# A decoder layer on one core: keys, values and both C products in another order on TensorE and VectorE

## The chip, the core and the metric

The kernel runs on one core of a Trainium2 chip. A core has five engines with a queue each, which work through their own instructions in order and meet only at semaphores: TensorE (PE) for matrix products into the eight PSUM banks, VectorE (DVE), ScalarE (ACT), GpSimd (POOL), and SyncE (SP), which here issues the transfers. TensorE's clock has two levels, 1.2 and 2.4 GHz. The metric is device time in microseconds (us), the median of several runs.

## The reference

One decoder layer over x of 8 x 256 tokens by 256 features, in three parts. The change lies in the first, which is the state-space mixer and the projections of the attention:

```python
x = _lin(x, w1); x = _depthwise_conv(x, conv_w, conv_b); x = jax.nn.silu(x)
x_delta = jax.nn.softplus(_lin(x, dl_w, dl_b))
A_bar = jnp.exp(-x_delta * _lin(x, A_w, A_b))
h = jnp.cumsum(_lin(x, B_w, B_b) * jnp.cumprod(A_bar, axis=1), axis=1)
ssm_out = _lin(h, C_w, C_b) + _lin(x, D_w, D_b)
z = ssm_out * jax.nn.silu(_lin(ssm_out, w2))
out = ssm_out + _lin(z, w3)
...
x = x + _L0_attn_ref(_layernorm(x, axis=-1), ...)
x = x + _L0_xattn_ref(_layernorm(x, axis=-1), ctx_1024, ctx_1024, ...)   # q from x, k and v from the context
x = x + _L0_ffn_ref(_layernorm(x, axis=-1), ...)
```

## The kernel before

The kernel has three stages, one after the other with a barrier between them: the mixer and the projections to queries, keys and values (`mixer_and_projections`), the attention, and the output projection with routing and experts. Queries, keys and values go to DRAM at the end of the first stage and are loaded again by the second.

The first stage works in four blocks of 512 tokens (`NBLK`, i = 0 to 3), with 256 features as two halves of 128 partitions. Each fp32 operand is split in a high and a low part (fp32r), and `split_product` makes three matmuls of each product. ScalarE as a rule writes the high part with an ACTIVATE, and VectorE or GpSimd the low part by a subtraction. The block loop is a software pipeline, written out by hand for each engine: iteration i does the work of block i (`now`) and what is left of block i - 1 (`last`), and the queries of block i - 2. There is no planner: the order of the calls in these loops is the order of the instructions.

On TensorE an iteration has the twelve chunks of dl, A and B of block i through a ring of four banks, `direct`, `turn_x` and `w1` of the next block, `w2` of the last, `turn_c` (transposes of the context), and then the part that the change reorders: `w3(i - 1)`, whose 40 matmuls also add the mixer's sum by an identity; `keys(i)` (12 matmuls of 512 columns); `values(i)` (24 of 256); `mixed(i, 0)` and `mixed(i, 1)`, the two halves of the product with C (12 of 512 each); and `turn_q(i - 1)`, the transposes of the normalised x that becomes the query input. `queries(i - 2)` then follows in the next iteration, behind the first two chunks.

The other engines meet this part so:

- VectorE adds w3's product to x (`residual`), makes the statistics of the second layer norm (`statistics`), the low part of keys (`biased_low`), the normalised x (`normed`), adds the bias to values (`value`), makes the running sum over the product with C (`summed`, a scan) and the low part of the turned x (`x2_low`), which stands between the two halves of the sum.
- GpSimd makes the reciprocal root of the variance (`power`, L329). Then come the remainders of values for their split in three bf16 parts (`v_rest`, L359, and `v_third`, L363), and in the next iteration `ssm_sum` (L339) and `dmin` (L334).
- ScalarE makes the high part of keys (`k_high`), the first and second parts of values (`v_first`, `v_second`) and then the high part of the turned x (`x2_high`, L537). Its next exponential, `exp` (L467), waits for a chunk of the ring.

Banks 4 to 7 are used as two pairs in turn. Which pair a product takes follows from its place in the tuple `PAIRS`. Before a pair is written, the reader of what was in it before must be done, so the order of the products also says which waits stand ahead of each.

Of the kernel before, what the change touches and what calls it, by code (L numbers as in the profile page):

```python
# [15 lines left out]
B, L, D = 8, 256, 256  # L16
N = B * L
DC = D // P
# [148 lines left out]
PAIRS = ("Q", "T", "D", "W1", "W2", "TC", "W3", "K", "V", "C", "TQ")  # L167


def mixer_and_projections(nc, sems, c, x_sb, wo, bo, a, disp, qd, kd, vd):  # L170

    with ExitStack() as ctx:
# [71 lines left out]
        with nc.Block() as block:  # L244
# [385 lines left out]
            def _(pe):  # L630
# [54 lines left out]
                def mixed(i, m):  # L685
                    pe.wait_ge(S["gh"], HC * (i + 1))
                    pe.wait_ge(S["gl"], HC * (i + 1))
                    pe.wait_ge(S["kl"], DC * (i + 1))
                    split_product(pe, pair(i, "C", m)[:, :], products("C_w", m, (gh, gl))).then_inc(S["C"], 1)
# [11 lines left out]
                def w3(i):  # L701
# [3 lines left out]
                    pe.wait_ge(S["zl"], DC * (i + 1))  # L705
                    for n in range(2):
# [16 lines left out]
                def keys(i):  # L723
                    if i == 0:
                        split_done(pe, "WQ")
                    pe.wait_ge(S["ch"], DC * (i + 1))
                    pe.wait_ge(S["cl"], DC * (i + 1))
                    for m in range(DC):
                        split_product(pe, pair(i, "K", m)[:, :], products("WK", m, (xbh, xbl))).then_inc(S["k"], 1)

                def values(i):
                    ge(pe, S["x_out"], 2 * i)
# [17 lines left out]
                for i in range(NBLK + 2):  # L750
# [20 lines left out]
                    if now:  # L771
                        chunk(i, "B", 1)
                        chunk(i, "dl", 3)
                        chunk(i, "A", 3)
                        turn_c(i)
                        chunk(i, "B", 2)
                        chunk(i, "B", 3)
                    if last:
                        w3(i - 1)
                    if now:  # L780
                        keys(i)
                        values(i)
                        mixed(i, 0)
                    if last:
                        turn_q(i - 1)
                    if now:
                        mixed(i, 1)

            @block.vector
            def _(dve):  # L790
# [161 lines left out]
                for i in range(NBLK + 2):  # L952
# [43 lines left out]
                    if now:  # L996
# [4 lines left out]
                        weighted(i, 3)  # L1001
                    if last:
# [4 lines left out]
                    if now:  # L1007
                        biased_low(i, "K", bk, i)
                    if last:
                        normed(i - 1)  # L1010
                    if now:
                        value(i, 0)
                        value(i, 1)
# [791 lines left out]
```

## Time and profile before

| | us |
|---|---|
| median of 3 runs (lowest, highest) | 880.38 (880.03, 880.54) |
| the profiled execution | 886.03 |
| its span | 884.3 |
| TensorE busy in the span | 693.3 (78%) |
| VectorE, ScalarE, GpSimd busy | 578.6, 434.1, 370.6 |

The profile is one execution with the hardware profiler on. Its time is some 6 us above the median of the runs. "Span" runs from the first to the last instruction. The first stage fills the first 285 us of it, and the attention's first matmul is at 316.79 us. A row of the timeline gives start and length in us, engine, line, operation, output and inputs by the program's names, the shape, and how often it repeats; in brackets the idle time of the engine before it and the instruction that ended it. Matmuls are pipelined, so their starts are read, and not their ends.

### The profile page before, as it was taken

Reading aid. Unit: us, or ns where it says so; the run is one execution under the profiler, and the core shown is the slowest. Engines: PE = TensorE matmul, PEld = TensorE weight load, DVE = VectorE, ACT = ScalarE, POOL = GpSimd, SP = SyncE. Lnnn points to the kernel's source line nnn. Section 1 sums busy time; section 2 is a strip of 40 time slices with the busy share of each in tenths; the row PEclk is TensorE's granted clock in tenths of the full one; section 3 lists DMA queues with packets and bytes.
Section 4 is the critical chain, followed back from the end, with each engine's and each line's share of the span. In section 5 each row is a group of like instructions: output and inputs, shape, how many; then the busy total and the mean of one; then the engine's idle time right before and its main releaser. Section 6 shows DMA issues by size and latency. Waiting matters only on the chain. (4 is left out here: it accounts for less than half of the span.)

```text
span 884.3 us, 15113 instructions
## 1 busy us (share of the span) xinstructions
PE 693.3 (78%) x4776; PEld 607.0 (69%) x4792; DVE 578.6 (65%) x1269; ACT 434.1 (49%) x971; POOL 370.6 (42%) x338
## 2 busy tenths in 40 slices
PE   3767969799765068898888676516999999999992
PEld 2556858688644046666666575516999999999992
DVE  6574466574753049999999767713777787777741
ACT  4554646535341047777777512103565565555641
POOL 1429456364420300000000156671466866866756
PEclk9788979989997569999999856556999999999997
DMA  9002005511030242121111052215044354251213
GB/s 302 19 25 86 1 24 212 190 65 69 23 111 30 90 139 51 47 46 47 47 46 41 19 197 73 70 43 186 2 136 113 60 147 131 39 146 19 28 22 41
DMA packets 54858, 70.36 MB, mean 80 GB/s; under 512 B 10843, under 2 KB 45542, under 8 KB 54800
## 3 DMA queue, kind: packets, MB, share of 16 engines
q1 hardware_dynamic: 45584, 61.82, 21.7%
q0 software_dynamic: 9216, 7.81, 6.2%
q8 instruction: 31, 0.51, 0.2%
q14 instruction: 27, 0.22, 0.1%
HBM read 42.57 MB, written 28.79 MB: 81 GB/s over the span
## 5 line engine op out<-in xcount | busy, mean ns | idle before, releaser
L1115 ACT ACTIVATE a_pr<-a_scores,a_nm 128x128 f32<-128x128 f32 (+1 forms) x256 | 90.5, 426 | 81.9 <-DVE a_nm L1187 78.6
L1695 DVE SCALAR_TENSOR_TENSOR w_v<-w_th,w_bank 128x324 f32<-128x324 f32 x128 | 63.0, 492 | 70.5 <-ACT w_th L1425 69.2
L1564 PE MATMUL w_bank<-w_w2h,w_hh 128*108 128x256 f32 x384 | 108.5, 283 | 0.5 <-POOL w_hl L1350 0.5
L1564 PE MATMUL w_bank<-w_w2h,w_hl 128*108 128x256 f32 x384 | 107.7, 280 | 0.0
L1564 PE MATMUL w_bank<-w_w2l,w_hh 128*108 128x256 f32 x384 | 107.4, 280 | 0.0
L1425 ACT ACTIVATE w_th<-w_bank 128x324 f32<-128x324 f32 x128 | 56.6, 442 | 100.0 <-PE w_bank L102 99.8
L1350 POOL TENSOR_TENSOR w_hl<-w_v,w_hh 128x324 fp32r<-128x324 f32 x64 | 56.4, 882 | 91.4 <-ACT w_hh L1431 91.4
L1184 DVE TENSOR_REDUCE a_mx<-a_scores 128x2 f32<-128x512 f32 (+1 forms) x96 | 65.5, 682 | 35.6 <-remote 34.1
L1366 POOL IOTA w_x<- 128x16 uint32 x1 | 0.2, 190 | 208.0 <-POOLq L1078 208.0
L102 PE MATMUL w_bank<-w_xh,w_w1h 128*128 128x324 f32 x256 | 81.1, 317 | 1.1 <-ACT w_xh L1420 1.1
L102 PE MATMUL w_bank<-w_xh,w_w1l 128*128 128x324 f32 x256 | 80.8, 316 | 0.0
L102 PE MATMUL w_bank<-w_xl,w_w1h 128*128 128x324 f32 x256 | 80.6, 315 | 0.0
L1150 PE MATMUL a_turned<-c_ident,a_pr 128*128 128x128 f32 x384 | 61.1, 282 | 21.0 <-ACT a_pr L1115 19.7
L1671 DVE TENSOR_TENSOR w_w2l<-w_s,w_w2h 128x256 fp32r<-128x256 f32 x64 | 74.3, 1160 | 2.2
L102 PE MATMUL a_scores<-a_kxh,a_qh 128*128 128x512 f32 x96 | 47.3, 493 | 33.5 <-DMA a_vs<-vd 33.5
L1192 DVE TENSOR_TENSOR a_pl<-a_turned,a_ph 128x512 f16<-128x512 f32 x96 | 66.4, 692 | 6.5 <-ACT a_ph L1122 5.7
L1564 PEld LDWEIGHTS w_bank<-w_w2h,w_hh 128*108 128x108 f32 x384 | 65.9, 172 | 0.7 <-issue 0.7
L1431 ACT ACTIVATE w_hh<-w_v 128x324 fp32r<-128x324 f32 x128 | 60.4, 472 | 12.0 <-DVE w_v L1695 11.2
L1564 PEld LDWEIGHTS w_bank<-w_w2l,w_hh 128*108 128x108 f32 x384 | 66.0, 172 | 0.0
L1564 PEld LDWEIGHTS w_bank<-w_w2h,w_hl 128*108 128x108 f32 x384 | 65.8, 171 | 0.0
L1150 PEld LDWEIGHTS a_turned<-c_ident,a_pr 128*128 128x128 f32 x384 | 43.6, 143 | 30.9 <-ACT a_pr L1115 27.2
L102 PE MATMUL m_bank<-m_sh,m_wh 128*128 128x512 f32 x112 | 48.0, 429 | 19.5 <-ACT m_sh L458 6.9
(230 smaller groups left out, 2031.2 us busy)
## 6 DMA issues: line engine op xcount, KB each, us to landing
w_s<-in_L_ffn_w SPq DMA_DIRECT2D x16, 1024.0 KB, 5.9
disp<-c_blank SPq DMA_DIRECT2D x8, 658.1 KB
w_rows<-disp SPq DMA_DIRECT2D x8, 658.1 KB
vd<-m_vs SPq DMA_DIRECT2D x4, 816.0 KB, 3.7
a_vs<-vd SPq DMA_DIRECT2D x1, 3264.0 KB, 11.8
g_x<-in_x SPq DMA_DIRECT2D x4, 512.0 KB, 7.7
m_cin<-in_ctx SPq DMA_DIRECT2D x4, 512.0 KB, 5.0
kd<-m_qkh SPq DMA_DIRECT2D x4, 512.0 KB, 2.9
```

The costliest lines, as they stand in the source:

```text
L102: mm = pe.matmul(out, a, b, start=first and n == 0, stop=last and n == 3 * len(parts) - 1)
L1115: ins = act.activation(pr[:, u % 2, j * n:(j + 1) * n], sbank[u % 3][:, j * n:(j + 1) * n], ACT.Exp, bias=nm[:, u, j:j + 1], scale=SCALE)
L1150: mm = pe.transpose(tbank[u % 3][:, j * P:(j + 1) * P], pr[:, u % 2, j * P:(j + 1) * P], c["ident"][:, :])
L1184: dve.tensor_reduce(mx[:, u, 0:nh], sbank[u % 3][:, :].rearrange("p (h k) -> p h k", h=nh), AX.X, ALU.max).then_inc(S["mx"], 1)
L1192: dve.tensor_tensor(pl[:, u % 3, :], tbank[u % 3][:, :], ph[:, u % 3, :], ALU.subtract)\
L1350: pool.tensor_tensor(hl[:, g % 3, half(1)], v[:, n % 4, :], hh[:, g % 3, half(1)].bitcast(F32), ALU.subtract)\
L1366: pool.iota(x3[:, :, TOK:TOK + 1].bitcast(U32), [[P, NT], [1, 1]], base=0, channel_multiplier=1)\
L1425: act.activation(th[:, n % 2, :], hb[n % 3][:, 0:HALF], ACT.Tanh, scale=0.5).then_inc(F["th"], 1)
L1431: act.activation(hh[:, g % 3, half(u)], v[:, n % 4, :], ACT.Copy).then_inc(F["hh"], 1)
L1564: mm = pe.matmul(eb[t // 2][0:SP_, (t % 2) * D:(t % 2 + 1) * D], a[:, g % 3, s], w2_piece(b, f), start=f == 0 and t % 2 == 0 and n == 0, s ...
L1671: dve.tensor_tensor(w2_piece(w2l, f), w2_piece(s2[e % 2], f), w2_piece(w2h, f).bitcast(F32), ALU.subtract)\
L1695: dve.scalar_tensor_tensor(v[:, n % 4, :], th[:, n % 2, :], 1.0, hb[n % 3][:, 0:HALF], ALU.add, ALU.mult).then_inc(F["v"], 1)
```

## The change

Four edits in the first stage. The tuple `PAIRS` names keys and values ahead of w3's product. On TensorE `keys(i)` and `values(i)` stand ahead of `w3(i - 1)`, and `mixed(i, 1)` ahead of `turn_q(i - 1)`. On VectorE the low part of keys and the two value sums stand ahead of the residual, and the normalisation follows the statistics directly. Waits follow the banks: C waits for the value sums (`vf`) and no longer for the low part of keys (`kl`), w3's product waits for `kl`, keys wait for `z`, and values no longer wait for `x_out`.

```diff
--- before.py
+++ after.py
@@ -164,7 +164,7 @@
 HIGH_ORDER = ("w1", "dl_w", "A_w", "B_w", "D_w", "WQ", "w2", "WO")
 LOW_VECTOR = ("w1", "dl_w", "A_w", "B_w", "D_w")
 LOW_GPSIMD = ("WQ", "w2", "WO")
-PAIRS = ("Q", "T", "D", "W1", "W2", "TC", "W3", "K", "V", "C", "TQ")
+PAIRS = ("Q", "T", "D", "W1", "W2", "TC", "K", "V", "W3", "C", "TQ")
 
 
 def mixer_and_projections(nc, sems, c, x_sb, wo, bo, a, disp, qd, kd, vd):
@@ -685,7 +685,7 @@
                 def mixed(i, m):
                     pe.wait_ge(S["gh"], HC * (i + 1))
                     pe.wait_ge(S["gl"], HC * (i + 1))
-                    pe.wait_ge(S["kl"], DC * (i + 1))
+                    pe.wait_ge(S["vf"], 2 * (i + 1))
                     split_product(pe, pair(i, "C", m)[:, :], products("C_w", m, (gh, gl))).then_inc(S["C"], 1)
 
                 def w2(i):
@@ -703,6 +703,7 @@
                         pe.wait_ge(S["identr"], 1)
                     pe.wait_ge(S["zh"], DC * (i + 1))
                     pe.wait_ge(S["zl"], DC * (i + 1))
+                    pe.wait_ge(S["kl"], DC * upto(i + 2))
                     for n in range(2):
                         for j in range(2):
                             tok = slice((2 * n + j) * P, (2 * n + j + 1) * P)
@@ -725,11 +726,11 @@
                         split_done(pe, "WQ")
                     pe.wait_ge(S["ch"], DC * (i + 1))
                     pe.wait_ge(S["cl"], DC * (i + 1))
+                    ge(pe, S["z"], DC * i)
                     for m in range(DC):
                         split_product(pe, pair(i, "K", m)[:, :], products("WK", m, (xbh, xbl))).then_inc(S["k"], 1)
 
                 def values(i):
-                    ge(pe, S["x_out"], 2 * i)
                     pe.wait_ge(S["dx"], DC * (i + 1))
                     for n in range(2):
                         for j in range(2):
@@ -775,16 +776,16 @@
                         turn_c(i)
                         chunk(i, "B", 2)
                         chunk(i, "B", 3)
+                    if now:
+                        keys(i)
+                        values(i)
                     if last:
                         w3(i - 1)
                     if now:
-                        keys(i)
-                        values(i)
                         mixed(i, 0)
+                        mixed(i, 1)
                     if last:
                         turn_q(i - 1)
-                    if now:
-                        mixed(i, 1)
 
             @block.vector
             def _(dve):
@@ -999,18 +1000,17 @@
                         weighted(i, 2)
                         running(i, 3)
                         weighted(i, 3)
+                    if now:
+                        biased_low(i, "K", bk, i)
+                        value(i, 0)
+                        value(i, 1)
                     if last:
                         residual(i - 1, 0)
                         residual(i - 1, 1)
                         dve.wait_ge(S["x_out"], 2 * i)
                         statistics(st2, mom2, ve2, TPB * (i - 1), TPB * i)
-                    if now:
-                        biased_low(i, "K", bk, i)
-                    if last:
                         normed(i - 1)
                     if now:
-                        value(i, 0)
-                        value(i, 1)
                         summed(i, 0)
                     if i == NBLK - 1:
                         last_sum(i, 0)
```

TensorE in the program, from the end of block 1's last chunks on (iteration i = 2): what it issues at the head of each product, before. `m_xbh` is the context's high part, `m_zh` that of z, `m_gh` that of the scan that is multiplied with C, `m_xn` the normalised x, `m_xah` the query input, `m_sh` the input of the chunks.

```order
L715 MATMUL m_bank4<-m_wh,m_zh 128x256 [waits m_zl,m_zh]
...
L102 MATMUL m_bank6<-m_xbh,m_wh 128x512 [waits m_cl,m_ch]
...
L102 MATMUL m_bank4<-m_wh,m_xbh 128x256 [waits m_dx,m_x_out]
...
L102 MATMUL m_bank6<-m_gh,m_wh 128x512 [waits m_kl,m_gl,m_gh]
...
L636 MATMUL m_bank4<-c_ident,m_xn 128x128 [waits m_xn2,m_vf]
...
L102 MATMUL m_bank7<-m_gh,m_wh 128x512 [waits m_kl,m_gl,m_gh]
...
L102 MATMUL m_bank6<-m_xah,m_wh 128x512 [waits m_hs,m_xl2,m_xh2]
```

And now:

```order
L102 MATMUL m_bank4<-m_xbh,m_wh 128x512 [waits m_z,m_cl,m_ch]
...
L102 MATMUL m_bank6<-m_wh,m_xbh 128x256 [waits m_dx]
...
L716 MATMUL m_bank4<-m_wh,m_zh 128x256 [waits m_kl,m_zl,m_zh]
...
L102 MATMUL m_bank6<-m_gh,m_wh 128x512 [waits m_vf,m_gl,m_gh]
...
L102 MATMUL m_bank7<-m_gh,m_wh 128x512 [waits m_vf,m_gl,m_gh]
...
L636 MATMUL m_bank4<-c_ident,m_xn 128x128 [waits m_xn2,m_vf]
...
L102 MATMUL m_bank6<-m_xah,m_wh 128x512 [waits m_hs,m_xl2,m_xh2]
```

The product with w3 has moved behind keys and values, and the second C product ahead of the query transposes. Two chunks stand between the last two rows of each list, as before.

VectorE in iteration i = 3, before: `L900` is the residual, `L810` the statistics, `L915` the low part of keys, `L907` the normalisation, `L922` the value sums, `L894` the scan over C, `L820` the low part of the query input.

```order
L900 TENSOR_TENSOR g_x<-m_bank6,g_x 128x512 [waits m_w3]
...
L810 BN_STATS m_st2<-g_x 128x6 [waits m_x_out]
...
L915 SCALAR_TENSOR_TENSOR m_qkl<-m_bank4,m_bk,m_qkh 128x512 [waits m_kh]
...
L907 TENSOR_SCALAR m_xn<-g_x,m_mom2,m_rstd2 128x256 [waits m_xT,m_rstd]
...
L922 TENSOR_TENSOR m_vf<-m_bank6,m_bv 128x512 [waits m_v3,m_v]
...
L894 SCALAR_TENSOR_TENSOR m_ssm<-m_bank4,m_dx 128x256 [waits m_wlp,m_z,m_dx,m_ssml,m_C]
...
L820 TENSOR_TENSOR m_xal<-m_bank6,m_xah 128x512 [waits m_xh2]
...
L894 SCALAR_TENSOR_TENSOR m_ssm<-m_bank5,m_dx 128x256 [waits m_wlp,m_z,m_dx,m_ssml,m_C]
```

The same place now, with lines one higher:

```order
L916 SCALAR_TENSOR_TENSOR m_qkl<-m_bank6,m_bk,m_qkh 128x512 [waits m_kh]
...
L923 TENSOR_TENSOR m_vf<-m_bank4,m_bv 128x512 [waits m_v3,m_v]
...
L901 TENSOR_TENSOR g_x<-m_bank6,g_x 128x512 [waits m_w3]
...
L811 BN_STATS m_st2<-g_x 128x6 [waits m_x_out]
...
L908 TENSOR_SCALAR m_xn<-g_x,m_mom2,m_rstd2 128x256 [waits m_xT,m_rstd]
...
L895 SCALAR_TENSOR_TENSOR m_ssm<-m_bank4,m_dx 128x256 [waits m_wlp,m_z,m_dx,m_ssml,m_C]
...
L821 TENSOR_TENSOR m_xal<-m_bank6,m_xah 128x512 [waits m_xh2]
...
L895 SCALAR_TENSOR_TENSOR m_ssm<-m_bank5,m_dx 128x256 [waits m_wlp,m_z,m_dx,m_ssml,m_C]
```

Keys' low part and the value sums have moved ahead of the residual. The second scan still stands behind the low part of the query input. The queues of ScalarE, GpSimd and SyncE are the same in both kernels.

## Rows read from the trace of the kernel before

**Rows 1.** The page, part 2: TensorE's granted clock in 40 slices, in tenths.
```profile
PEclk9788979989997569999999856556999999999997
```

**Rows 2.** Timeline of TensorE, block 2: first matmul of each product in turn.
```profile
178.59 0.55 PE L715 MATMUL m_bank<-m_wh,m_zh 128*128 128x256 f32 x1 [5.83 <-POOL m_zl L343]
...
185.27 0.39 PE L102 MATMUL m_bank<-m_xbh,m_wh 128*128 128x512 f32 x1
...
188.05 0.28 PE L102 MATMUL m_bank<-m_wh,m_xbh 128*128 128x256 f32 x1
...
190.90 0.39 PE L102 MATMUL m_bank<-m_gh,m_wh 128*128 128x512 f32 x1
...
193.71 1.04 PE L636 MATMUL m_bank<-c_ident,m_xn 128*128 128x128 f32 x8
...
197.39 0.40 PE L102 MATMUL m_bank<-m_sh,m_wh 128*128 128x512 f32 x1
...
200.20 0.41 PE L102 MATMUL m_bank<-m_xah,m_wh 128*128 128x512 f32 x1
```

**Rows 3.** Timeline of VectorE and GpSimd, low parts of context and z, block 2.
```profile
177.16 1.29 DVE L820 TENSOR_TENSOR m_xbl<-m_bank,m_xbh 128x512 fp32r<-128x512 f32 x2 [3.75 <-ACT m_xbh L512]
...
175.95 2.49 POOL L343 TENSOR_TENSOR m_zl<-m_z,m_zh 128x512 fp32r<-128x512 f32 x2
```

**Rows 4.** Timeline of VectorE, 185 to 199 us.
```profile
185.47 0.69 DVE L900 TENSOR_TENSOR g_x<-m_bank,g_x 128x512 f32<-128x512 f32 x1 [1.62 <-PE m_bank L720]
...
189.73 1.38 DVE L907 TENSOR_SCALAR m_xn<-g_x,m_mom,m_rstd 128x256 f32<-128x256 f32 x4
...
195.96 1.29 DVE L820 TENSOR_TENSOR m_xal<-m_bank,m_xah 128x512 fp32r<-128x512 f32 x2 [0.78 <-ACT m_xah L537]
...
197.59 1.27 DVE L894 TENSOR_TENSOR_SCAN m_ssm<-m_bank,m_dx 128x256 f32<-128x256 f32 x2 [0.34 <-PE m_bank L102]
```

**Rows 5.** Timeline of GpSimd, 188 to 195 us.
```profile
188.57 1.04 POOL L329 TENSOR_TENSOR m_rstd<-m_ve,c_mhalf 128x4 f32<-128x4 f32 x1 [1.25 <-DVE m_ve L119]
192.49 2.28 POOL L359 TENSOR_TENSOR m_vf<-m_vf,m_vs 128x512 f32<-128x512 f32 x2 [2.87 <-ACT m_vs L527]
```

**Rows 6.** Timeline of ScalarE, 182 to 206 us.
```profile
182.83 0.63 ACT L484 ACTIVATE m_gh<-m_acc 128x512 fp32r<-128x512 f32 x1 [0.50 <-DVE m_acc L873]
...
194.79 0.66 ACT L531 ACTIVATE m_vs<-m_vf 128x512 bf16<-128x512 f32 x1 [0.45 <-POOL m_vf L359]
195.35 1.06 ACT L537 ACTIVATE m_xah<-m_bank 128x512 fp32r<-128x512 f32 x2
...
204.61 0.69 ACT L467 ACTIVATE m_e<-m_bank,m_dlb 128x512 f32<-128x512 f32 x1 [0.71 <-PE m_bank L102]
```

**Rows 7.** Timeline of TensorE, C and query products of blocks 1 and 3.
```profile
135.25 0.39 PE L102 MATMUL m_bank<-m_gh,m_wh 128*128 128x512 f32 x1
...
144.54 0.41 PE L102 MATMUL m_bank<-m_xah,m_wh 128*128 128x512 f32 x1
...
242.07 0.39 PE L102 MATMUL m_bank<-m_gh,m_wh 128*128 128x512 f32 x1
...
250.17 0.47 PE L102 MATMUL m_bank<-m_xah,m_wh 128*128 128x512 f32 x1 [1.45 <-DVE m_ssm L894]
```

**Rows 8.** Timeline of VectorE, block 3: the two sums of scan and direct part.
```profile
246.37 1.23 DVE L806 TENSOR_TENSOR m_ssm<-m_ssm,m_dx 128x512 f32<-128x512 f32 x1
...
250.06 0.69 DVE L806 TENSOR_TENSOR m_ssm<-m_ssm,m_dx 128x512 f32<-128x512 f32 x1
```

**Rows 9.** Windows from S on: stretch, its length, busy engines, clock, transfers.
```profile
122.06:128.35 6.29, 6.29 (x30) 6.29 (x31) 4.66 (x7) 2.94 (x5) 2.97 (x3) 0.51 0.01 3
...
178.59:182.95 4.36, 4.36 (x20) 4.36 (x21) 3.95 (x6) 2.42 (x5) 1.58 (x1) 0.51 0.01 4
...
230.17:234.20 4.03, 4.03 (x21) 4.03 (x22) 3.79 (x6) 1.26 (x2) 1.25 (x1) 0.58 0.01 2
```

**Rows 10.** Timeline of VectorE and TensorE: end of the stage, start of the attention.
```profile
284.00 0.75 DVE L915 SCALAR_TENSOR_TENSOR m_qkl<-m_bank,m_bq,m_qkh 128x512 fp32r<-128x512 f32 x1 [0.78 <-ACT m_qkh L544]
...
316.79 0.76 PE L102 MATMUL a_scores<-a_kxh,a_qh 128*128 128x512 f32 x1 [33.55 <-DMA a_vs<-vd]
```

## The prediction

> **What bounds the kernel now.** I read the page first, then the timeline of each engine from 120 to 285 us, since the change touches only the four blocks of the first stage. The clock row of the page shows that this stage is not full: TensorE's granted clock dips in it again and again [rows 1]. The timeline shows a repeating pattern. In block 2 TensorE stands still until 178.59 us, released by GpSimd's last low part of z, and then runs without a gap: product with w3 to 185.27, keys to 188.05, values to 190.90, first C product to 193.71, query transposes, second C product, then two chunks of the next block at 197.39 and the query product at 200.20 [rows 2]. I call the first matmul of such a stretch S and the start of C in the old order W. In blocks 1 and 2 TensorE stays gapless beyond the query product, and ScalarE's next exponential waits for the chunk behind it (204.61, released by PE) [rows 6]. So a microsecond lost between S and the query product is lost for the block. From the third chunk on the block is a chain over ScalarE, VectorE and GpSimd that moves rigidly with its start. After block 3 the query product of block 2 waits outright for VectorE's scan (250.17, idle 1.45) [rows 7], and everything to the end of the stage is serial; attention's first matmul comes 32 us after the last low query part [rows 10], behind stores, a barrier and loads, which move with it.
>
> **What could start sooner: nothing.** Keys and values now go first in the stretch. Keys need the context's low part; the product with w3 needed z's low part. In block 2 VectorE ends the first at 177.16 + 1.29 = 178.45, GpSimd the second at 175.95 + 2.49 = 178.44 [rows 3]. S stays where it is (to 0.05 us), and the idle time ahead of it is not touched. The new wait of keys for z is met: z's low part is made from z. The work from S to W is the same 76 matmuls in another order, so W stays too: 178.59 to 190.90 = 12.31 us [rows 2].
>
> The new wait of w3's product for the low part of keys: the pair of banks that keys fill is the one w3 takes next. ScalarE evicts keys only behind its last copy of g, which ends 182.83 + 0.63 = 183.46, S + 4.87 [rows 6]; two evictions at the 0.69 of the same form [rows 6], and one low part at about the 0.69 of VectorE's 128x512 from a bank [rows 4], with handovers, give S + 7.0. The w3 product takes 6.68, of which 4.36 at half the clock [rows 2, 9], so at full clock 2.32 + 2.18 = 4.5, and it would start at W - 4.5 = S + 7.8. Behind it are queued both C products and the transposes; the margin is 0.8 us. Cost 0 to 0.5, taken 0. The C products now wait for the value sums, which are made while w3's product runs: nothing.
>
> **What becomes later.** The end of w3's product moves from S + 6.68 to W (190.90). It starts this chain, with the spans of block 2:
> - residual, statistics, variance on VectorE, then the power on GpSimd: from the product's end at 185.27 to 188.57 + 1.04 = 189.61 [rows 2, 4, 5], 4.34 us. So W + 4.35.
> - GpSimd's queue is unchanged, and in it the power stands AHEAD of the two value remainders. In the old order these waited for values and began at 192.49, long after the power [rows 5]. Now values are ready first and sit behind the power: 2.25 for the two [rows 5], W + 6.6.
> - ScalarE's second value part waits for the second remainder, and the copies of the turned query input stand behind it: 194.79, then 195.35; VectorE's low parts of the same 195.96 to 197.25 [rows 4, 6]. From the remainders' end (194.75) to the low parts' end 2.5: W + 9.1.
> - VectorE makes the second scan behind these low parts, 1.27 [rows 4]: W + 10.4. The query product waits for it.
>
> In the old order that scan waited only for the second C product, and the query product began at W + 9.30 in block 2 and W + 9.29 in block 1 [rows 2, 7]. TensorE could have it at W + 9.3 now too: C, C, transposes, two chunks are the same work. The transposes alone are checked separately: the last normalised tile is ready at W + 4.35 + 1.38 = W + 5.8 [rows 4], and two C products of 2.81 end at W + 5.6 [rows 2]: 0.1 to 0.2, which disappears in the later wait. So each of blocks 1 and 2 loses 10.4 - 9.3 = 1.1 us. GpSimd's first minimum for the next block comes 2.4 later, but the exponential that waits for TensorE comes only about 1.3 later, and the next one, behind TensorE's third chunk, 1.1.
>
> Block 3 has no chunks behind it. There the query product began at 250.17 - 242.07 = W + 8.10 [rows 7]. Between the scans VectorE also has a sum over two SBUF tensors, 1.23 beside GpSimd's value parts and 0.69 without [rows 8]. It would now start at W + 7.0, where GpSimd again makes those parts (W + 6.6 to 8.9), so I take 1.23: it ends at 8.3, 0.35 past the point at which the first low part could start. W + 10.75, a loss of 2.65. A page of the Trainium skill, "SBUF — State Buffer", section "Who interferes with whom", says that a VectorE instruction with two SBUF inputs contends with a GpSimd one that reads SBUF, under an exclusive lock. The pair of durations agrees.
>
> What is gained: the keys' store leaves sooner, and nothing waits for it; the second C product ends 0.8 sooner (the transposes no longer lie ahead of it), and that is what the longer chain hides.
>
> **The sum.** 1.1 + 1.1 + 2.65 = 4.85 us. The profiled execution took 886.03 us (span 884.3) and would take 890.9; the median of the runs is 880.38, so the same sum gives 885.2.
>
> **The clock.** The stretches at 1.2 GHz after S are 6.3 us long in block 1 and about 4.4 and 4.0 in the others [rows 9]; each costs up to half its length, whichever product lies in it. The change moves work, not the gap before S, so I take 0. Bounds: without any such stretch W could come no sooner than S + 7.0 + 4.5 = S + 11.5 because of the wait for keys; against 13.19, 12.31 and 11.90 now [rows 2, 7, 9] that is at most 1.7 + 0.8 + 0.4 = 2.9 gained. At the long stretch in all three, (6.3 - 4.4)/2 + (6.3 - 4.0)/2 = 2.1 lost. The Trainium skill, "TensorE: Matmul & The Clock Gate", section "What's actually happening", adds that the gate's phase varies from run to run and that one should not fit to a cold count; three lengths in one trace agree, and the term stays 0.
>
> **Rivals.**
> 1. The chain costs nothing (not slower). Place: GpSimd between the power and the remainders of blocks 1 to 3. If the power were ready in time, or the second scan did not have to follow the low parts, the query product would come at W + 9.3, and in block 3 0.8 sooner than now, since C ends 0.8 sooner. It decides for this side once the low parts end before W + 8.0, instead of 9.1. Time 880.38 - 0.8 = 879.6; with half of the clock's possible gain 878.2. Against it: the sequence stands in the queues, with measured spans. 7 in 100.
> 2. The chain costs what I say, and the clock falls in the holes it opens: TensorE idles 1.1 in two blocks and, in block 3, from about W + 6.7 to W + 10.75, where it idled 1.45 before. The query product and the one with w2, some 2.8 us each, could run at half speed: +2.8 to +5.6, of which I take 2.8: 888.0. For it: each longer idle ahead of S ends at half clock [rows 9]. Against it: it needs the hole to be counted as idle. 13 in 100.
> 3. The normalisation on VectorE now meets the remainders on GpSimd. The page on SBUF named above says that a `tensor_scalar` can enter a mode that takes the shared ports, and then one blocks the other. As a mechanism here: the remainders or the normalised tiles come up to 1.38 later [rows 4], three times up to 1.3: +2 to +4, 888. Against it: 1.38 for four tiles of 256 columns, 0.35 each, is no faster than a plain pass of that shape by the 0.69 for 512 from a bank [rows 4]. 7 in 100.
> 4. The chain is shorter than I sum it, or the clock gives back some: a loss of 1 to 3 us, 882.5. 18 in 100.
>
> The forecast itself, 885.2, has 55 in 100, with a range of its own of 883.5 to 887. What a measurement of this kernel tells from no change is 0.2%, 1.8 us. Slower by more: 55 + 13 + 7 and most of rival 4, 0.89. Within: 0.08. Faster: 0.03, rival 1 with clock luck. The range, from the floor of chain less clock (880.4 + 4.85 - 2.9 = 882.3) to rivals 2 and 3: 882 to 888.3.
>
> **What would show it.** Right: S of block 1 unchanged near 122; keys, values, w3's product, C, C, transposes without a gap; the value remainders directly behind the power on GpSimd; the query product waiting about 1 us for VectorE's scan in blocks 1 and 2, and nearly 4 us in block 3; S of blocks 2 and 3 about 1.1 and 2.2 later; the last query part 4.85 later, and equal distances behind it. Wrong: no idle time ahead of the query product; a gap between values and w3's product released by the low part of keys; gaps ahead of S that shrink; remainders that run before the power.

## The result and the profile after

| | before | after |
|---|---|---|
| median (lowest to highest), us | 880.2 (879.84 to 880.54), 4 runs | 901.74 (899.95 to 903.35), 4 runs |
| the profiled execution, us | 886.03 | 902.52 |
| its span, us | 884.3 | 900.8 |

The changed kernel takes 1.0244 times as long, with a 95% interval of 1.0222 to 1.0266. It is slower, as forecast, but by 21.5 us in the medians where the prediction had 4.85. The profiled pair differs by 16.5 us, mostly since before's profiled execution lay 5.8 above its own median. Below, traces are compared with traces and medians with medians.

The whole loss of the traces lies in the first stage. The last product of queries starts at 298.12 us, against 278.81 before, the last low part at 303.42 against 284.00 [rows 10], and attention's first matmul at 335.76 against 316.79 [rows 10]. That is 19.3, 19.4 and 19.0 us. What follows the attention's first matmul is 2.5 us shorter in the later trace, which makes the 16.5 of the pair; a comparison of two single traces is uncertain by some microseconds in total, and is read below place by place.

The timeline of TensorE in block 2 answers to [rows 2]. Columns: start and length in us, engine, line, operation, output and inputs, shape and count, idle time before it and what ended it.

```profile
182.79 0.76 PE L102 MATMUL m_bank<-m_xbh,m_wh 128*128 128x512 f32 x1 [5.78 <-ACT m_xbh L512]
188.04 0.42 PE L102 MATMUL m_bank<-m_wh,m_xbh 128*128 128x256 f32 x1
191.25 0.28 PE L716 MATMUL m_bank<-m_wh,m_zh 128*128 128x256 f32 x1
195.91 0.40 PE L102 MATMUL m_bank<-m_gh,m_wh 128*128 128x512 f32 x1
201.69 0.30 PE L636 MATMUL m_bank<-c_ident,m_xn 128*128 128x128 f32 x1
202.76 0.33 PE L636 MATMUL m_bank<-c_ident,m_xn 128*128 128x128 f32 x1 [0.77 <-DVE m_xn L908]
203.92 0.33 PE L636 MATMUL m_bank<-c_ident,m_xn 128*128 128x128 f32 x1 [0.83 <-DVE m_xn L908]
205.07 0.76 PE L636 MATMUL m_bank<-c_ident,m_xn 128*128 128x128 f32 x5 [0.83 <-DVE m_xn L908]
205.59 0.56 PE L102 MATMUL m_bank<-m_sh,m_wh 128*128 128x512 f32 x1
210.02 0.39 PE L102 MATMUL m_bank<-m_xah,m_wh 128*128 128x512 f32 x1
```

Keys, values, w3's product and the C products follow one another as forecast. S to W, by the prediction's names, is 182.79 to 195.91. But the query product starts at W + 14.11, not W + 10.4. Two things stand between. The eight transposes wait for VectorE's normalised tiles one by one, so that the chunks start 9.68 behind C and not 6.5. And the two chunks take 4.43 instead of 2.81. The reason for the first is on VectorE and GpSimd, in the same stretch (they answer to [rows 4] and [rows 5]):

```profile
196.11 0.69 DVE L901 TENSOR_TENSOR g_x<-m_bank,g_x 128x512 f32<-128x512 f32 x1 [1.65 <-PE m_bank L721]
200.29 4.72 DVE L908 TENSOR_SCALAR m_xn<-g_x,m_mom,m_rstd 128x256 f32<-128x256 f32 x4 [1.15 <-POOL m_rstd L329]
204.94 1.26 DVE L895 TENSOR_TENSOR_SCAN m_ssm<-m_bank,m_dx 128x256 f32<-128x256 f32 x2
206.12 1.26 DVE L821 TENSOR_TENSOR m_xal<-m_bank,m_xah 128x512 fp32r<-128x512 f32 x2
207.30 1.25 DVE L895 TENSOR_TENSOR_SCAN m_ssm<-m_bank,m_dx 128x256 f32<-128x256 f32 x2
```

```profile
199.22 1.04 POOL L329 TENSOR_TENSOR m_rstd<-m_ve,c_mhalf 128x4 f32<-128x4 f32 x1 [7.65 <-DVE m_ve L119]
200.23 2.32 POOL L359 TENSOR_TENSOR m_vf<-m_vf,m_vs 128x512 f32<-128x512 f32 x2
202.51 2.36 POOL L363 TENSOR_TENSOR m_vs<-m_vf,m_vs 128x512 bf16<-128x512 f32 x2
206.27 1.28 POOL L339 TENSOR_TENSOR m_ssm<-m_ssm,m_dx 128x512 f32<-128x512 f32 x1 [1.41 <-DVE m_ssm L895]
```

Four normalised tiles that took 1.38 before [rows 4] take 4.72. They fill the very time in which GpSimd makes its four value remainders (200.23 to 204.87), while GpSimd keeps its pace (2.32 and 2.36, before 2.28 [rows 5]). By source line, all 16 tiles of a run, with lowest, median and highest ns, before and then after:

```profile
L907 DVE TENSOR_SCALAR m_xn<-g_x,m_mom,m_rstd x16: 404/409/414, 134.1 to 275.6; 128x256 f32<-128x256 f32 x16
```

```profile
L908 DVE TENSOR_SCALAR m_xn<-g_x,m_mom,m_rstd x16: 406/1235/1251, 139.1 to 294.9; 128x256 f32<-128x256 f32 x16
```

In block 2 a transpose follows each tile, at 201.69, 202.76, 203.92 and 205.07: the tiles come some 1.16 apart, which is the length of one remainder (2.32 for two). One tile gets in per GpSimd instruction. The last four of the 16 lie in the serial end, without remainders beside them, which is why the lowest of the row is still 406.

The reason for the second is the clock, in the windows of the two chunks of blocks 1 and 2 and of block 3's query product (us, busy time of TensorE, its weight loads, VectorE, ScalarE, GpSimd; granted clock; DMA share; GB/s), after and then the same two kinds of stretch before:

```profile
144.34:148.78 4.44, 4.44 (x16) 3.50 (x15) 2.96 (x6) 3.59 (x7) 2.68 (x3) 0.62 0.88 305
205.59:210.02 4.43, 4.43 (x16) 3.49 (x15) 2.96 (x6) 1.62 (x3) 2.67 (x3) 0.61 0.51 189
265.35:270.80 5.45, 5.45 (x12) 3.77 (x12) 1.33 (x2) 0.69 (x1) 0.00 (x0) 0.51 0.01 2
```

```profile
197.39:200.20 2.81, 2.81 (x13) 2.26 (x12) 1.27 (x2) 0.69 (x1) 2.14 (x3) 1.00 0.80 296
250.17:253.00 2.83, 2.83 (x12) 2.14 (x12) 1.02 (x2) 0.69 (x1) 0.00 (x0) 1.00 0.59 217
```

The same matmuls run at a granted clock of 0.61 and 0.51 instead of 1.00, behind transposes that came in drops. In block 3 the whole query product is at the lower level. Its start there, and that of the last query product, after and then before:

```profile
265.35 0.76 PE L102 MATMUL m_bank<-m_xah,m_wh 128*128 128x512 f32 x1 [3.04 <-DVE m_ssm L895]
298.12 0.76 PE L102 MATMUL m_bank<-m_xah,m_wh 128*128 128x512 f32 x1 [1.46 <-ACT m_xah L537]
```

```profile
278.81 0.77 PE L102 MATMUL m_bank<-m_xah,m_wh 128*128 128x512 f32 x1 [1.46 <-ACT m_xah L537]
```

The stage as a sum, in starts on TensorE; Q is the query product that follows C:

| us | before | after | difference |
|---|---|---|---|
| S of block 1 | 122.06 | 121.72 | -0.34 |
| S to W, blocks 1, 2, 3 | 13.19, 12.31, 11.90 | 12.95, 13.12, 11.91 | +0.58 |
| W to Q, blocks 1, 2, 3 | 9.29, 9.30, 8.10 | 14.11, 14.11, 13.53 | +4.82, +4.81, +5.43 |
| Q of block 3 to the last Q | 28.64 | 32.77 | +4.13 |
| Q of blocks 1 and 2 to the next S | 34.05, 29.97 | 34.01, 29.89 | -0.12 |

### The profile page after: what moved, and what is told of

Same layout as the page of the kernel before. It is cut to its first block and busy times, and to the rows that moved or that the text cites. A ratio compares the mean times of both kernels' runs of the same rounds, so it can differ in the third digit from the quotient of the medians.

```text
span 900.8 us, 15111 instructions
## 1 busy us (share of the span) xinstructions
PE 699.8 (78%) x4776; PEld 607.8 (67%) x4792; DVE 587.8 (65%) x1269; ACT 434.1 (48%) x971; POOL 370.5 (41%) x338
```

## Experiments

Each kernel is timed beside the kernel before on the same chip; "before" in this section is that run's median. Where nothing else is said the edit is to the changed kernel, and W and Q are the starts as above. My theory A after the trace: VectorE's tiles are held out by GpSimd's instructions, and the late transposes and cold chunks follow from that. Rivals: B, the tiles are slow for their place in VectorE's order (behind the statistics and the power), whatever GpSimd does; C, the moved C product does it all.

### The remainders ahead of the power on GpSimd

```diff
-                    if last:
-                        power(3 + i, ve2, rstd2, slice(TPB * (i - 1), TPB * i))
                     if now:
                         v_rest(i, 0)
                         ...
                         v_third(i, 1)
+                    if last:
+                        power(3 + i, ve2, rstd2, slice(TPB * (i - 1), TPB * i))
```

> The changed kernel, with the value remainders and third parts ahead of the power in GpSimd's queue. Theory A (a normalisation tile on VectorE cannot run beside a GpSimd instruction; each of the four waits one out): GpSimd is idle while the tiles are made, so they take 1.4 us instead of 4.7, the transposes follow C without a gap, TensorE does not fall to half clock behind them, and the query product comes 9.3 to 9.6 us after the first C product instead of 14.1. Time 879 to 882 us. Theory B (the tiles are slow by their place in VectorE's order, behind the statistics, whatever GpSimd does): the tiles stay at 4.7 us, only ScalarE's second value parts come sooner, which nothing waited for in the end: 899 to 902 us.

Measured: 891.59 (890.13 to 892.54), before 882.0, ratio 1.0109 (1.0086 to 1.0132). The mechanism came as theory A had it. GpSimd does its remainders and then the power, and VectorE's tiles, in their place in the changed kernel's order, are back at their length:

```profile
132.89 2.28 POOL L363 TENSOR_TENSOR m_vs<-m_vf,m_vs 128x512 bf16<-128x512 f32 x2
138.08 1.04 POOL L329 TENSOR_TENSOR m_rstd<-m_ve,c_mhalf 128x4 f32<-128x4 f32 x1 [2.92 <-DVE m_ve L119]
```

```profile
139.16 1.38 DVE L908 TENSOR_SCALAR m_xn<-g_x,m_mom,m_rstd 128x256 f32<-128x256 f32 x4 [1.15 <-POOL m_rstd L329]
```

W to Q is 9.51 in block 1 (134.77 to 144.28). Theory B falls. The time, though, is 9.6 above the upper end of what I expected. The trace has 7.0 of it at the last Q. In block 3 W comes at S + 13.12 (S at 230.79) where before had 11.90, and Q at W + 10.19 where before had 8.10, and starts at half clock:

```profile
243.91 0.40 PE L102 MATMUL m_bank<-m_gh,m_wh 128*128 128x512 f32 x1
254.10 0.77 PE L102 MATMUL m_bank<-m_xah,m_wh 128*128 128x512 f32 x1 [3.53 <-DVE m_ssm L895]
285.82 0.77 PE L102 MATMUL m_bank<-m_xah,m_wh 128*128 128x512 f32 x1 [1.46 <-ACT m_xah L537]
```

And from that Q to the last one 31.72 pass instead of 28.64: the first seven matmuls of this query product run at the lower clock, and the whole product with w2 does (granted clock 0.50, 5.46 us).

### The remainders behind the tiles

```diff
                     if now:
+                        ge(pool, S["xn2"], TPB * i)
                         v_rest(i, 0)
```

> The changed kernel, with GpSimd's value remainders held until the four normalised tiles are made. Theory A: tiles 1.4 us; remainders start 5.8 us after the start of C, so the query input's low parts end at 10.6 and the second scan at 11.9; the query product at about 12 instead of 14.1 in blocks 1 and 2, the transposes without gaps and the chunks behind them at full clock. Some 2 us per block better than the changed kernel: 893 to 897 us. Theory B: tiles stay at 4.7, remainders come 4.7 later as well: slower than the changed kernel, 908 us or more.

Measured: 898.72 (898.24 to 899.64), ratio 1.0194 (1.0172 to 1.0215), 1.7 above the upper end. GpSimd's first remainder is released by VectorE's last tile, and all 16 tiles take 404 to 413 ns. VectorE, then GpSimd:

```profile
139.51 1.38 DVE L909 TENSOR_SCALAR m_xn<-g_x,m_mom,m_rstd 128x256 f32<-128x256 f32 x4 [1.16 <-POOL m_rstd L329]
```

```profile
140.97 2.28 POOL L359 TENSOR_TENSOR m_vf<-m_vf,m_vs 128x512 f32<-128x512 f32 x2 [1.50 <-DVE m_xn L909]
```

Q of block 1 stands at 147.07, W + 11.94: the chain power, tiles, remainders, ScalarE's copies, scan is now serial, 1.5 longer than the W + 10.4 of the prediction (1.38 of tiles ahead of the remainders). So the two orders without an overlap both have short tiles, whichever of the two goes first.

### The C products in their old order, in the changed kernel

```diff
                         mixed(i, 0)
-                        mixed(i, 1)
                     if last:
                         turn_q(i - 1)
+                    if now:
+                        mixed(i, 1)
```

> The changed kernel, with the query transposes back between the two C products (one part of the change undone). Theory A: the tiles still take 4.7 us and now TensorE reaches the transposes 2.8 us earlier, with only one C product in front, so it stands longer before them and the second C product comes after: the scan behind it ends at about 14.1 after the start of C and the query product at 15.5. 904 to 908 us, slower than the changed kernel. Theory C (the loss comes from moving the second C product): the loss goes away in large part, 885 to 890 us.

Measured: 908.04 (906.8 to 910.15), ratio 1.0302 (1.0273 to 1.033), at the upper end of what was expected. The tiles stay at a median of 1233 ns. Now nothing covers them: the transposes stand directly behind one C product and wait 2.78 and then 0.77, 0.69 and 0.68. The second C product behind them starts at half clock, and Q of block 1 comes at W + 17.16, 1.7 later than I had expected. By the two ratios the moved C product helps in the changed kernel, by some 5 us (1.0302 against 1.0244); theory C falls.

### The C products in the new order, alone, in the kernel before

```diff
                     if now:
                         mixed(i, 0)
+                        mixed(i, 1)
                     if last:
                         turn_q(i - 1)
-                    if now:
-                        mixed(i, 1)
```

> The kernel before, with only the second C product moved ahead of the query transposes. Theory A: GpSimd and the normalisation do not meet, tiles 1.4 us; the query input's copies come 2.8 us later and the scan behind them ends about 9.3 after the start of C, just where the query product stood; in block 3 about 1.2 us are lost. 880 to 882 us. Theory C (the loss comes from moving the second C product): most of the 21 us, 895 or more.

Measured: 888.43 (886.11 to 889.31), ratio 1.0073 (1.0046 to 1.01). That is 6 us above "no change": missed. The tiles are at 407 ns. In blocks 1 and 2 Q comes at W + 9.51 and W + 9.50, 0.2 later than before. In block 3 the window from S to W is 1.2 longer, at clock 0.77 where the same window before had 0.86 (first the experiment, then before):

```profile
231.19:244.28 13.09, 13.09 (x77) 12.57 (x78) 9.98 (x25) 3.27 (x5) 3.95 (x3) 0.77 0.02 8
```

```profile
230.17:242.07 11.90, 11.90 (x76) 11.37 (x77) 9.89 (x25) 3.27 (x5) 3.96 (x3) 0.86 0.02 7
```

Then Q comes at W + 9.49 (+1.4) behind an idle time of 2.84, and the serial end is 2.95 longer: the query product and the one with w2 both run in good part at the lower clock (4.6 us each instead of 2.8 and 3.0). Nearly all of the loss on the trace, 5.5 of 6.5 us, stands in block 3 and behind it, and 4.1 of it lies in these two stretches of lower clock. That S to W of 13.1 belongs to this order is not shown: with one and the same order on TensorE the changed kernel has 11.91 there, and the first two experiments have 13.12 each.

### Does any GpSimd instruction hold the tiles? Two probes in the kernel before

```diff
+                    if last and now:
+                        for n in range(2):
+                            pool.tensor_tensor(scrap[:, n * BLK:(n + 1) * BLK],
+                                wh[:, 0:BLK].bitcast(F32), wh[:, BLK:2 * BLK].bitcast(F32), ALU.subtract).then_inc(S["scrap"], 1)
+                        pool.wait_ge(S["scrap"], 2 * i)
```

> The kernel before, with two subtractions of 128x512 on GpSimd (SBUF to a scratch tile that nobody uses) directly behind the power in iterations 1 to 3, where GpSimd was idle and VectorE makes the normalised tiles. Theory A: each waits for a GpSimd instruction while one runs; of the four tiles two are held for about 1.2 us each, so the four take 3 to 3.6 us instead of 1.4 in blocks 1 to 3; the time is up by 0 to 3 us, since the transposes come 2.8 us after C's start there. Theory B (the tiles are slow from their place in the order): 1.4 us still.

In the second probe the two subtractions are replaced by `pool.memset(scrap[:, :], 0.0)` twice, over 1536 columns of bf16, which read nothing:

> As the probe with subtractions, but two memsets of 1536 bf16 columns on GpSimd, which write and read nothing, some 1.3 us each. If the tiles and GpSimd meet at a port that both need for any access, the four tiles take 3 to 3.6 us here as well. If they meet only where both read SBUF, they take 1.4 us.

Measured: 889.69 and 890.3 (one run each, before 882.61). VectorE's order is that of before in both. The tiles of block 1 and the probes beside them, first with subtractions, then with memsets:

```profile
132.36 3.24 DVE L912 TENSOR_SCALAR m_xn<-g_x,m_mom,m_rstd 128x256 f32<-128x256 f32 x4
132.22 2.59 POOL L414 TENSOR_TENSOR m_scrap<-m_wh 128x512 bf16<-128x512 f32 x2
```

```profile
132.77 3.46 DVE L912 TENSOR_SCALAR m_xn<-g_x,m_mom,m_rstd 128x256 f32<-128x256 f32 x4
132.60 2.84 POOL L415 MEMSET m_scrap<- 128x1536 bf16 x2
```

Two foreign GpSimd instructions lengthen the four tiles from 1.38 to 3.24 and 3.46, the longest single tile to 1378 and 1542 ns. The first was expected at 3 to 3.6. GpSimd's instructions beside them are the cause; which data they touch, and whether they read at all, did not matter here. The page "SBUF — State Buffer" of the Trainium skill, section "Who interferes with whom", gives this as its single rule: VectorE's second pair of ports is GpSimd's only pair, and it is an exclusive lock. Both probes agree with it, the second for writes alone. The two single times lie 7.1 and 7.7 us above before's median, where I had expected 0 to 3 for the first; on the traces the last Q is 4.4 and 5.2 later. The second C product and block 3's Q come later, and the product with w2 runs in good part at the lower clock (4.58 and 4.42 us instead of 3.03). One run of each kernel does not bound what the probes cost in time; the lengths of the tiles are what they show.

### Filling TensorE's wait

Is the second part, the cold chunks, a consequence of the hole? Twelve matmuls of 512 columns whose result nobody reads, ahead of the transposes of blocks 1 to 3:

```diff
                     if last:
+                        if now: fill(i - 1)  # waits for x_out of block i - 1, then 12 matmuls of 512 columns into the TQ pair
                         turn_q(i - 1)
```

> The changed kernel, with 12 matmuls of 512 columns on constant weights, whose result is overwritten, between the second C product and the query transposes of blocks 1 to 3, where TensorE stands for 3 us in pieces. They add 2.8 us of TensorE's work per block and change nothing for VectorE and GpSimd. Theory A with the clock as its second half (the tiles that wait for GpSimd leave TensorE idle, and the two chunks or the query product behind the transposes then run at half clock, 4.4 us for two chunks instead of 2.8): the chunks take 2.8 us, the query product comes about 12.8 us after C's start instead of 14.1, and the time falls by 2 to 5 us, to 897 to 900, although work is added. Without the clock's part (the chunks are slow for another reason): the added work costs nothing or up to 1.5 us, 901 to 905. The tiles stay at 4.7 us by either.

Measured: 901.35 (898.38 to 903.42), before 882.61, ratio 1.0219 (1.0196 to 1.0242): 0.0025 under the changed kernel's, about 2.2 us, and 1.35 above the expected range. The local effect is as forecast: W to Q falls from 14.11 to 12.83 in both blocks, and the two chunks run at full clock (granted 1.00, 3.10 us):

```profile
140.54 2.91 PE L659 MATMUL m_bank<-m_wh 128*128 128x512 f32 x12
143.29 0.49 PE L636 MATMUL m_bank<-c_ident,m_xn 128*128 128x128 f32 x3
144.12 0.77 PE L636 MATMUL m_bank<-c_ident,m_xn 128*128 128x128 f32 x5 [0.34 <-DVE m_xn L915]
144.64 0.48 PE L102 MATMUL m_bank<-m_sh,m_wh 128*128 128x512 f32 x1
147.74 0.48 PE L102 MATMUL m_bank<-m_xah,m_wh 128*128 128x512 f32 x1
```

The tiles are still at 1248 ns. The intervals of the two ratios overlap, so the gain in total time is not certain; that the hole made the chunks cold is, since they run at full clock in both blocks once it is filled.

The same in the serial end, where the changed kernel lost 4.13: fillers only ahead of block 3's query product, the last products with w2 and w3, and the last transposes.

> The changed kernel, with TensorE's idle stretches filled only behind block 3: 12, 12, 18 and 20 matmuls ahead of the query, w2, w3 products and the last transposes. Theory: of the 9.7 us that the end of the stage is longer than before, some 4 are the two products that ran at half clock behind the longer wait, and what before itself lost there comes on top: tiles stay at 4.7, the time falls by 6 to 10 us to 892 to 896. Rival (the end is long by waits alone): 900 to 902.

Measured: 898.29 (897.55 to 898.73), before 881.31, ratio 1.0189 (1.0172 to 1.0206), against 1.0244 for the changed kernel. The last Q comes at 292.68 instead of 298.12, 5.4 earlier; the time falls by some 4.8 us, and I had expected 892 to 896. The first fillers cost something themselves: the 12 ahead of the query product ran at half clock (5.32 us) and pushed it to W + 15.29, from W + 13.53. From there to the last Q it is 25.86 instead of 32.77.

### What the clock costs the kernel before

The edit, condensed; the comments say where each filler stands:

```diff
+                def fill(n, out):
+                    for q in range(n):
+                        pe.matmul(out[:, :], wh[:, 0:P], wh[:, 0:BLK], start=q == 0, stop=q == n - 1)
                 ...
+                    if i + 1 == NBLK: fill(20, banks[0])      # ahead of turn_q's wait
+                    if i + 1 == NBLK: fill(12, banks[0])      # ahead of w2's waits
+                    pe.wait_ge(S["z"], DC * (i + 1))          # i + 1 < NBLK
+                    fill(18, pair(i + 1, "W3", 0))            # ahead of w3's waits, every block
+                    fill(6, banks[0])                         # ahead of block 3's query product
```

> The kernel before, with matmuls on constant weights in TensorE's idle stretches of the first stage: 18 of 512 columns ahead of w3's product in blocks 1 to 3 (3.9 us at full clock, in gaps of 4.6 to 5.8), and 6, 12, 18 and 20 ahead of the query, w2, w3 products and the transposes behind block 3. Theory (the clock costs up to half of the stretches at 1.2 GHz): S to the start of C falls from 13.2, 12.3 and 11.9 to about 10.3 us each, which is 6 us, and the serial end is 3 to 5 us shorter: 870 to 874 us. Rival (the added matmuls push the work behind them, or the blocks are bound by the other engines anyway): 880 us or more.

Measured: 874.86 (874.55 to 877.21), before 882.61, ratio 0.9918 (0.9894 to 0.9942). This beats both kernels. The order is that of before; only the waits are filled. In block 1, to be held against S to W of 13.19 in [rows 2, 7, 9]:

```profile
117.28 4.55 PE L660 MATMUL m_bank<-m_wh 128*128 128x512 f32 x18
122.11 0.36 PE L728 MATMUL m_bank<-m_wh,m_zh 128*128 128x256 f32 x1 [0.29 <-POOL m_zl L343]
132.84 0.47 PE L102 MATMUL m_bank<-m_gh,m_wh 128*128 128x512 f32 x1 [0.22 <-DVE m_qkl L933]
```

```profile
122.11:132.84 10.73, 10.51 (x76) 9.81 (x77) 10.16 (x22) 4.32 (x7) 6.49 (x5) 1.00 0.01 2
```

S is where it was, since the same low part of z ends the wait, and W comes 10.73 behind it at clock 1.00 (10.78 and 10.36 in blocks 2 and 3). The last Q is at 271.07, 7.7 earlier. So before, too, pays about 8 us for its holes through the clock. The Trainium skill, "TensorE: Matmul & The Clock Gate", section "What's actually happening", puts the ramp at under 1% of a typical kernel's span. The 0.8% that the fillers gave back here agree with that as a total, and are still more than the whole effect that I had forecast.

Fillers in block 0 too (22, 26 and 20 matmuls):

> The kernel before with the same added matmuls as in the filled kernel before, and 22, 26 and 20 more in TensorE's three idle stretches of block 0 (6.9, 6.7 and 4.9 us), behind which the chunks, B and keys start at half clock. If block 0 is bound by TensorE behind these stretches as the later blocks are, 3 to 6 us less than the filled kernel: 868 to 872 on a chip where before is 880 to 882. If it is bound by weight loads and the other engines, the same as that: 874.

Measured: 874.86 (873.85 to 875.99), before 881.31, ratio 0.9918 (0.9901 to 0.9934). The granted clock of the early slices rises from 7 and 8 tenths to 9, and neither the time nor S of block 1 moves (122.02, against 122.11): the clock of these stretches does not bound block 0.

### The new order at its best

The first experiment's order (remainders ahead of the power) together with fillers in all the places where TensorE waits:

> The changed kernel with the remainders ahead of the power (tiles at 1.4 us) and with TensorE's idle stretches filled as in the filled kernel before: 18 matmuls ahead of keys, 14, 12, 18, 20 in the serial end. If what is left of the loss in that kernel (9.6 us against before) is the clock and the wait of the query product in block 3 (10.2 us after C's start against 8.1), then with the clock held this lies 2 to 3 us above the filled kernel before: 876 to 879. If the order itself costs more, 882 or above. If it is the better order once the clock is held, under 873.

Measured: 881.49 (879.66 to 882.3), before 881.31, ratio 0.9998 (0.9988 to 1.0007), missed by 2.5. With tiles short and the clock held, the new order is still 6.6 us behind the old one with fillers. The reason stands on TensorE and VectorE of block 1:

```profile
128.24 0.36 PE L726 MATMUL m_bank<-m_wh,m_zh 128*128 128x256 f32 x1 [1.18 <-DVE m_qkl L934]
```

```profile
126.69 1.41 DVE L934 SCALAR_TENSOR_TENSOR m_qkl<-m_bank,m_bk,m_qkh 128x512 fp32r<-128x512 f32 x2 [1.27 <-ACT m_qkh L521]
```

S is 121.16 here. The product with w3 waits 1.18 for the low part of keys, which is ready at 128.10, S + 6.9. S to W is 11.8 in all three blocks, where the old order has 10.4 to 10.8, and block 3's Q comes at W + 10.2 instead of W + 8.1. In the changed kernel itself that wait is hidden by the half clock after S.

## Why the prediction was wrong

"Slower" came out, but for the larger part not for the reason that was given: the forecast chain accounts for 2.65 of the 19.3 us on the traces at most, and the rest was either held at nothing or left to rivals. Point by point, in its own order.

- **S unchanged, no gap to W.** Right. S of block 1 moved by -0.34, and no gap stands ahead of w3's product.
- **The wait of w3's product for the low part of keys, S + 7.0, cost 0.** Right for this kernel: in block 2 the low part is ready at 189.76, S + 6.97, and the product starts at 191.25. The margin is 1.5 and not 0.8, since keys and values, which now stand where the half clock falls, take until then. With the clock held (above) the same wait costs 1.2 us in each block, so the 0 held only because of the slow start.
- **The chain over GpSimd's queue.** The mechanism was there and its first steps right: the power ends at 200.26, W + 4.35, exactly the step forecast; the first pair of remainders follows directly and ends at 202.55, W + 6.64, where W + 6.6 was forecast. Its later steps, the low parts and the second scan, came behind the late tiles: the low parts end at W + 11.5 and not at W + 9.1.
- **"The last normalised tile is ready at W + 4.35 + 1.38 = W + 5.8."** This step failed. The tiles took 4.72, and the last was ready at 205.01, W + 9.1. The prediction had put the tiles and the remainders at the same place in time, W + 4.35, on two engines, and priced the tiles from a row in which they ran alone. For one sum in block 3 it had allowed for GpSimd beside VectorE; for the tiles it had not. The late transposes then take the place of the late low parts as what sets Q: 3.2 us in each of blocks 1 and 2. Removing the overlap in either direction gives tiles of 0.41 (first two experiments), and adding foreign GpSimd work to the old order gives slow ones (the two probes), so this cause is shown.
- **Rival 3 named exactly this and was given 7 in 100.** The argument against it was that 0.35 for 256 columns "is no faster than a plain pass", so that VectorE could not be using the shared ports. Duration does not show that: the tiles have no gain in speed to be seen and are held all the same. Whether they run in a mode with two pairs of ports, or are held for another reason, was not tried. The rival's own price, up to 1.38 per block, was also too small: the tiles wait out GpSimd's instructions, not their own length, so the price is four steps of 1.16 instead of four of some 0.33, 4.72 - 1.38 = 3.3.
- **There was a row in the trace of before.** At the program's start four tiles of the same form follow the first power, beside one GpSimd memset, and take 2.00 instead of 1.38; the longest has 1031 ns. I had not looked for a place where this pair of instructions met. First GpSimd, then VectorE:

```profile
8.09 0.95 POOL L367 MEMSET m_ypad<- 128x1032 f32 x1
```

```profile
8.16 2.00 DVE L801 TENSOR_SCALAR m_xn<-g_x,m_mom,m_rstd 128x256 f32<-128x256 f32 x4 [0.80 <-POOL m_rstd L329]
```

- **The clock, taken as 0, with bounds of -2.9 and +2.1.** This is the second failed term. The bounds counted only the stretches behind S. The holes among the transposes cost 1.6 per block in blocks 1 and 2 (chunks of 4.43 instead of 2.82). Not all of that could have been had back: VectorE's second scan ended at W + 12.64, so Q could not have come before that. In block 3 they put the query product at half clock (5.45 instead of 2.83), and the distance from Q to the last Q grew by 4.1: 2.4 up to the product with w2, 1.5 from there to w3's. Rival 2 had this mechanism for block 3 only, at 2.8 to 5.6. Together the clock is some 7 us of the 19.3; filling the holes gives back 1.3 in each of two blocks, and 5.4 at the end, where before too had lost some.
- **The sum over SBUF tensors in block 3 at 1.23.** Wrong, the other way: at 262.13 it takes 0.69, since by then GpSimd was done. It is a small term.
- **Moving the C product, costed at a gain of 0.8 that hides.** It gains in the changed kernel (some 5 us) and loses in the old one (6.4 in the medians), mostly behind block 3. In both, what counts is which hole it leaves or fills.

On the traces the 19.3 us divide so: held tiles 3.2 + 3.2 in blocks 1 and 2 and 2.8 in block 3 (13.53 less the forecast 10.75); the chain in block 3, by the prediction's own figure, 2.65; the clock 1.6 + 1.6 + 4.1; S of block 1 and S to W together 0.1. The split within block 3 is argued and not measured by itself. In blocks 1 and 2 the 1.1 forecast for the chain is hidden behind the tiles. In the medians, the remainders ahead of the power gave back 11.9 us of the 21.5 (1.0244 to 1.0109), with what clock followed from it. That edit took away the overlap and, with it, the chain of remainders behind the power. Where the overlap went and that chain stayed and grew by the tiles (second experiment), 4.4 us came back. What the overlap alone costs in the medians was not isolated. Open is why 9.6 us stay in the first of these. Its trace has 0.6 at S of block 3, 1.2 of S to W there, 2.1 of the late Q and 3.1 in the serial end, the same places as in the experiment that only moved the C product; the last of these goes with the lower clock, the wait behind the late Q was not taken away by an experiment, and the other 2.6 lie between medians and traces.

## What to carry to other kernels

After a reorder, go through each VectorE instruction that reads and writes only SBUF and ask what GpSimd does in the same microseconds; a duration from a row is good only for the neighbours that it had in that row. Search the trace for any place where the two already meet, and read the longest instance there, not the mean. And price a hole on TensorE twice, as idle time and as half clock on the work behind it; where the data come late anyway, filler matmuls in the wait give the second part back, as in the version at 874.86 us here.

## What the runs showed of the hardware that was not expected

- A `tensor_scalar` with two scalars per partition over 128x256 fp32, SBUF to SBUF, takes 409 ns alone and is held to 1235 ns beside a row of 128x512 GpSimd instructions of 1.16 us each, while these take 2.32 and 2.36 for two instead of 2.28 and 2.30. One VectorE instruction gets in per GpSimd instruction, and GpSimd loses next to nothing.
- A GpSimd memset, which reads nothing, holds the tiles like a subtraction does (3.46 and 3.24 for four, against 1.38).
- VectorE's low parts of the turned x, whose one input is a PSUM bank, are not held: two take 1.26 beside GpSimd's sum over SBUF (206.12 on VectorE, 206.27 on GpSimd), as they take 1.28 elsewhere.
- Filler matmuls from data at rest, 18 of 512 columns in a wait, keep the granted clock at 1.00 through the next 10.7 us, and did not delay the start behind them by more than 0.1 us in block 1 (122.11, before 122.06).
